# A second stage rewritten: tokens scattered into expert slots, one 4096-column tanh a step, sums shared by GpSimd and VectorE

## The chip, the core and the metric

One core of one Trainium2 chip. The metric is the device time of one execution in microseconds (us), median of several runs; lower is better. The engines are TensorE (PE in the profile; PEld is its weight load), VectorE (DVE), ScalarE (ACT), GpSimd (POOL) and the SyncE queue that issues transfers (SP).

## What is computed

Two layers over 2048 tokens (2 images of 32 x 32 positions) of 128 channels. The first is a 7 x 7 neighbourhood attention with a gate and a layer norm; the change does not touch how it is computed. The second, in two parts:

```
# additive attention, per image (L = 1024 keys, U = 32 units)
q = t @ Wt ; k = t @ Wx
h = tanh(q[:, :, None, :] + k[:, None, :, :] + bh)
e = h @ Wa + ba ;  a = softmax(e)
t = t + a @ layernorm(t)
# experts: E = 8, F = 512, capacity C = ceil(1.25 * 2048 / 8) = 320
x = layernorm(t) ; logits = x @ gate_w + gate_b
idx, prb = top-1 expert and its softmax probability
pos = rank of the token among those of its expert ; kept = pos < C
y = (relu(x @ w1[idx] + b1[idx]) @ w2[idx] + b2[idx]) * prb * kept
out = t + nan_to_num(y)
```

## The kernel before

The first layer runs in 32 half-block turns (`for rho in range(NR)`) and ends near 177 us. Then come 16 query blocks of 128 tokens, 8 for each image. The tanh of a block has 128 queries x 1024 keys x 32 units; four queries' units lie side by side in the 128 partitions, so that a block is 8 steps (`CH = 8`) of 4 x 1024 columns.

In a step, ScalarE's `hidden_units` does two tanh of 1024 columns straight from the keys, with the query as bias (L734), and one of 2048 columns (L736) whose sums GpSimd has prepared with two instructions of 1024 (L350, `key_query_sums`). TensorE's `energies` (L538) turns the step into energies: 8 f32 matmuls of 512 columns, each recorded as two. The keys of a block are staged by SP as copies in SBUF (`kcur`, `qcur`, `xcur`).

Blocks are pipelined. While block i makes its energies, block i-1 goes through softmax, transposes (L550), the product with the tokens (L561), the residual and the norm, and block i-2 through its experts: for each of the 8 steps one expert, with all 128 tokens of the block, four matmuls in (L575), a relu on VectorE (`hidden`, L1013), four matmuls out (L589) and a masked sum (`combine`, L1030). Every expert therefore sees every token, and a mask keeps one. The engines' programs are written out in order and meet by semaphores. Most blocks run in a hardware loop. The layer norm of the second image (`norm_part(1, ...)`, L851 to L871) runs on VectorE alongside the first block's tanh. `Chain` makes VectorE wait for its own last result. After the last energies the experts of the last three blocks run alone (`ahead`), with `finish` (L1037 to L1042) cleaning infinities and adding the residual.

## Time and profile before

| what | us |
|---|---|
| median of 3 runs | 794.61 (793.82 to 796.89) |
| the profiled execution | 795.25 |
| its span, first to last instruction | 793.0 |
| busy in the span: PE, DVE, ACT, POOL | 729.0, 530.6, 628.7, 292.0 |

The busy share is an average over three stages: the first layer, the 16 blocks, and a tail. In the rows below the number behind "x" is a count; a time in square brackets is idle time of the engine before the row and what ended it. [...]

### The profile page before, as it was taken

The numbers are of one execution on the slowest core, as the hardware profiler recorded it, in microseconds if no ns is written. First come the engines' busy times: TensorE is split into PE (matmuls) and PEld (weight loads), VectorE is DVE, ScalarE is ACT, GpSimd is POOL, SyncE is SP. The second block draws the span as 40 slices with busy tenths as digits, with TensorE's granted clock in tenths as the row PEclk, the third lists the DMA queues.
The fourth block names the chain that finished last, engine by engine and source line by source line (L and its number), as shares of the span: only waits on it lengthen the run. The fifth ranks groups of instructions, "written<-read, shape, count | busy, mean of one in ns | idle before, by whom it ended". The sixth has DMA issues, their size and how long they took to land.

```text
span 793.0 us, 16921 instructions
## 1 busy us (share of the span) xinstructions
PE 729.0 (92%) x6288; PEld 462.4 (58%) x6288; DVE 530.6 (67%) x1464; ACT 628.7 (79%) x661; POOL 292.0 (37%) x264
## 2 busy tenths in 40 slices
PE   6899998875698999999999999999999999999987
PEld 3666666651144666656665656656565656656686
DVE  2566798859725376675858576675858576675776
ACT  2367676659799998989999898989989898989500
POOL 1000000008545454545454454545454454545100
PEclk9799999999699999999999999999999999999999
DMA  9000000007001001010101001010101001010000
GB/s 323 12 2 2 1 2 2 1 11 310 1 1 55 30 26 58 0 57 0 57 0 57 29 28 57 0 57 0 57 0 57 19 38 57 0 57 0 3 5 7
DMA packets 11364, 29.38 MB, mean 37 GB/s; under 512 B 3264, under 2 KB 5312, under 8 KB 10688
## 3 DMA queue, kind: packets, MB, share of 16 engines
q1 hardware_dynamic: 11328, 28.91, 9.7%
q8 instruction: 22, 0.36, 0.2%
q14 instruction: 14, 0.11, 0.0%
HBM read 10.81 MB, written 1.05 MB: 15 GB/s over the span
## 4 chain that ended last, share of the span: by engine, by line
PE 61%; DVE 26%; issue 4%; ACT 3%; DVEq 0%; DMA 0%; SPq 0%; ACTq 0%
PE ps L538 19%; PE ps L589 14%; PE ps L575 10%; PE ps L561 4%; PE ps L413 3%; DVE hids L1013 3%; PE ps L426 2%; DVE sw L113 2%; PE ps L395 2%; DVE sw L114 2%; DVE nmin L954 2%; PE ps L550 2%; DVE arena L804 2%; DVE oha L992 2%; DVE sy L116 2%
## 5 line engine op out<-in xcount | busy, mean ns | idle before, releaser
L734 ACT ACTIVATE arena<-kcur,qcur 128x1024 f32<-128x1024 f32 x240 | 261.9, 1138 | 42.7 <-PE ps L538 42.6
L538 PE MATMUL ps<-arena,nwa 128*32 128x512 f32 x2048 | 252.2, 611 | 16.7 <-ACT arena L736 16.1
L350 POOL TENSOR_SCALAR early<-kcur,qcur 128x1024 f32<-128x1024 f32 x120 | 132.7, 1118 | 167.2 <-ACT arena L736 104.2
L589 PEld LDWEIGHTS ps<-arena,hids 128*128 128x128 f32 x1024 | 124.1, 191 | 93.6 <-issue 71.4
L350 POOL TENSOR_SCALAR tokens<-kcur,qcur 128x1024 f32<-128x1024 f32 x120 | 133.1, 1122 | 101.1 <-ACT arena L736 100.9
L589 PE MATMUL ps<-arena,hids 128*128 128x128 f32 x1024 | 146.4, 286 | 8.4 <-DVE hids L1013 7.0
L575 PE MATMUL ps<-xnT,arena 128*128 128x128 f32 x1024 | 136.5, 277 | 0.0
L1013 DVE TENSOR_TENSOR hids<-ps,nb 128x512 f32<-128x512 f32 x128 | 88.2, 689 | 67.6 <-PE ps L575 62.9
L575 PEld LDWEIGHTS ps<-xnT,arena 128*128 128x128 f32 x1024 | 124.4, 192 | 0.1
L538 PEld LDWEIGHTS ps<-arena,nwa 128*32 128x32 f32 x2048 | 54.5, 110 | 117.0 <-issue 82.1
L736 ACT ACTIVATE arena<-early 128x2048 f32<-128x2048 f32 x64 | 121.3, 1896 | 0.3 <-POOL early L350 0.3
L736 ACT ACTIVATE arena<-tokens 128x2048 f32<-128x2048 f32 x64 | 121.3, 1895 | 0.0
L1030 DVE SCALAR_TENSOR_TENSOR acc<-ps,msk,acc 128x128 f32<-128x128 f32 x112 | 39.1, 349 | 81.6 <-PE ps L589 78.3
L678 ACT ACTIVATE arena<-arena,mn 128x320 f32<-128x320 f32 (+1 forms) x128 | 62.7, 540 | 34.0 <-DVE mn L804 32.8
L350 POOL TENSOR_SCALAR early<-kT,tokens 128x1024 f32<-128x1024 f32 x8 | 11.4, 1438 | 174.7 <-DVE tokens L935 173.0
L804 DVE CUSTOM_DVE_ANT_0 arena<-ps,arena 128x320 f32<-128x320 f32 (+1 forms) x128 | 53.0, 470 | 16.1 <-PE ps L395 11.6
L413 PE MATMUL ps<-cst,arena 128*128 128x128 f32 x352 | 56.1, 292 | 3.5 <-ACT arena L685 3.5
L413 PEld LDWEIGHTS ps<-cst,arena 128*128 128x128 f32 x352 | 41.5, 150 | 13.5 <-ACT arena L685 6.3
L685 ACT ACTIVATE arena<-ps 128x512 f32<-128x512 f32 x56 | 33.0, 588 | 10.3 <-PE ps L413 10.3
L1041 DVE COPY_PREDICATED acc<-bad,fill 128x128 f32<-128x128 uint32 x48 | 36.1, 751 | 1.7
L561 PE MATMUL ps<-xcur,ptm 128*128 128x128 f32 x256 | 34.0, 276 | 0.0
L561 PEld LDWEIGHTS ps<-xcur,ptm 128*128 128x128 f32 x256 | 31.1, 192 | 0.4 <-issue 0.4
(133 smaller groups left out, 704.9 us busy)
## 6 DMA issues: line engine op xcount, KB each, us to landing
kcur<-kT SPq DMA_DIRECT2D x16, 512.0 KB, 2.9
xcur<-x_all SPq DMA_DIRECT2D x16, 512.0 KB, 3.2
arena<-in_w SPq DMA_DIRECT2D x2, 2048.0 KB, 11.1
arena<-in_inner SPq DMA_DIRECT2D x1, 1280.0 KB, 11.5
tokens<-in_xT SPq DMA_DIRECT2D x4, 256.0 KB, 6.4
arena<-in_top SPq DMA_DIRECT2D x1, 1024.0 KB, 7.4
arena<-in_bottom SPq DMA_DIRECT2D x1, 1024.0 KB, 15.7
out<-outs SPq DMA_DIRECT2D x16, 64.0 KB, 1.6
```

Source lines behind the costliest of these rows:

```text
L350: last = nc.gpsimd.tensor_scalar(kq_sum[s % 2][:, c, :], keys[:, :], queries[:, m:m + 1], 1.0, ALU.add, ALU.mult)
L413: last = nc.tensor.transpose(bank(to, g * P, (g + 1) * P), prob[r][:, g, c * P:(c + 1) * P], c_("ident"))
L538: last = nc.tensor.matmul(bank(2 * par + half)[c * U:(c + 1) * U, :], nwa[:, U - QPG - QPG * s:2 * U - QPG - QPG * s], hid_ring[s % 2][:, ...
L561: last = nc.tensor.matmul(bank(5, 0, C), ptm[:, k, :], xcur[par][:, k * C:(k + 1) * C], start=(k == 0), stop=(k == BPI - 1))
L575: last = nc.tensor.matmul(bank(0 if ahead and e % 2 else 6, c * P, (c + 1) * P), w1[:, e, c * P:(c + 1) * P], xnT[par][:, :], start=True, ...
L589: last = nc.tensor.matmul(bank(1 if ahead and e % 2 else 7, 0, C), hids[e % 2][:, c, :], w2[:, e, c, :], start=(c == 0), stop=(c == FC - 1))
L678: nc.scalar.activation(prob[r][:, g, 0:n], nlog[r][:, g, 0:n], ACT.Exp, bias=mn[r][:, g:g + 1], scale=-1.0).then_inc(p_ready, 1)
L734: nc.scalar.activation(hid_ring[s % 2][:, c, :], keys[:, :], ACT.Tanh, bias=queries[:, m:m + 1])
L736: nc.scalar.activation(hid_ring[s % 2][:, 2:4, :], kq_sum[s % 2][:, :, :], ACT.Tanh).then_inc(h_ready, 1)
L804: nc.vector.tensor_tensor_reduce(out=nlog[r][:, g, 0:n], in0=bank(g, 0, n), in1=btab[kind][:, 2 * g + r, :], scale=-1.0, scalar=3e38, op0= ...
L1013: nc.vector.tensor_tensor(hids[e % 2][:, :, :], bank(0 if ahead and e % 2 else 6).rearrange("p (c t) -> p c t", c=FC), nb1[:, e * FC:(e + ...
L1030: nc.vector.scalar_tensor_tensor(acc[:, :], out, w, acc[:, :], ALU.mult, ALU.add).then_inc(out_used, 1)
```

## The change

- Experts leave the block loop. Each block ends in a record of 272 columns a token (normed token, residual, 8 logits less their maximum, token number) and in a slot number (expert x 320 + rank). GpSimd scatters the record to its slot in a DRAM buffer of 2560 rows with one indirect transfer (`scatter`). SP has filled this buffer with blank records before.
- After the last block SP loads all slots back (4 transfers of 5 tiles of 128 slots), and the experts run once, each on its own 320 slots. GpSimd scatters the 20 tiles of results to the output rows; a blank slot's token number is out of bounds and writes nothing. SP has stored the residual rows to the output before.
- A step has one tanh of 4096 columns, in place in a ring of three buffers. All sums are made ahead: GpSimd the first 2.5 of the four 1024-column pieces, VectorE the last 1.5. Both read `k4`, both may start filling step t+3 when the energies of step t are done.
- The softmax sum comes from a column of ones beside the tokens; least and copy of the energies are one VectorE instruction; both blocks' energies use the same two PSUM banks, so the next block waits for `least_ready`. The logits and counts are f32.
- The loops over blocks are written out in full.

```diff
+T = NB * CH
 # gpsimd
-                for c in range(2):
-                    m = (2 + c) * CH + s
-                    last = nc.gpsimd.tensor_scalar(kq_sum[s % 2][:, c, :], keys[:, :], queries[:, m:m + 1], 1.0,
-                                                   ALU.add, ALU.mult)
+                else:
+                    pool.wait_ge(h_used, t - 2)
...
+                for c in range(3):
+                    n = L if c < 2 else L // 2
+                    m = i * U + c * CH + s
+                    last = nc.gpsimd.tensor_scalar(ring[t % 3][:, c, 0:n], k4[:, img * L:img * L + n], q4[:, m:m + 1],
+                                                   1.0, ALU.add, ALU.mult)
+                last.then_inc(pool_sums, 1)
...
+            for t in range(T):
+                i, s = divmod(t, CH)
+                if s == 6 and i >= 2:
+                    scatter(i - 2)
+                if t + 2 < T:
+                    key_query_sums(t + 2)
 # tensor
+                if s == 0 and i:
+                    pe.wait_ge(least_ready, i)
...
+            def first_product(e):
+                pe.wait_ge(xeT_ready, 2 * (e // 2) + 2)
                 for c in range(FC):
...
+                    nc.tensor.matmul(bank(c, 0, CAP), w1[:, e, c * P:(c + 1) * P], xeT[:, e * CAP:(e + 1) * CAP],
+                                     start=True, stop=True).then_inc(w1_done, 1)
...
+                for k, row, at, n in parts_of(e):
+                    to = slot_bank(k)
...
+                    for c in range(FC):
+                        last = nc.tensor.matmul(to[row:row + n, :], h[e % 2][:, c, at:at + n], w2[:, e, c, :],
+                                                start=(c == 0), stop=(c == FC - 1))
 # scalar
-                for c in range(2):
-                    m = c * CH + s
-                    nc.scalar.activation(hid_ring[s % 2][:, c, :], keys[:, :], ACT.Tanh, bias=queries[:, m:m + 1])
-                act.wait_ge(sum_ready, CH * i + s + 1)
-                nc.scalar.activation(hid_ring[s % 2][:, 2:4, :], kq_sum[s % 2][:, :, :], ACT.Tanh).then_inc(h_ready, 1)
+            def hidden_units(t):
+                act.wait_ge(pool_sums, t + 1)
+                act.wait_ge(dve_sums, t + 1)
+                nc.scalar.activation(ring[t % 3], ring[t % 3], ACT.Tanh).then_inc(h_ready, 1)
 # vector
+                for c in range(2, QPG):
+                    lo = L // 2 if c == 2 else 0
+                    m = i * U + c * CH + s
+                    last = nc.vector.tensor_scalar(ring[t % 3][:, c, lo:L], keys[:, lo:L], q4[:, m:m + 1], None, ALU.add)
+                last.then_inc(dve_sums, 1)
...
+            key_query_sums(0)
+            key_query_sums(1)
+            dve.wait_ge(y_ready, NB)
+            for t in range(T):
...
+                if t < 4:
+                    for part in range(4 * t, 4 * t + 4):
+                        norm_part(1, part)
...
+                if p >= 1 and s == 1:
+                    turned_normed(p - 1)
+                if p >= 1 and s == 3:
+                    route(p - 1)
+                if p >= 0 and s == 3:
+                    turned_main(p)
+                if p >= 1 and s == 5:
+                    slotted(p - 1)
+                if p >= 0 and s == 6:
+                    attended(p)
+                if p >= 0 and s == 7:
+                    normed(p)
+                if p >= 0 and s == 0:
+                    least(p)
+                if t + 2 < T:
+                    key_query_sums(t + 2)
 # sync
+            sp.wait_ge(h_used, T)
+            for i in range(2):
+                sp.wait_ge(scattered[i], 16 * NB // 2)
+            for q in range(NE // 2):
...
+                sp.dma_start(xe[:, q * n:(q + 1) * n, :], src).then_inc(ld_xe[q], 16)
```

After the experts' products, VectorE's `rectified` (L1153) does half of the relu, ScalarE the other half, and `slots_out` (L1164 to L1172) weighs, cleans and adds the residual for 2 or 3 tiles of slots at once.

How the order changes, first on GpSimd in the loop over blocks. Before, two steps of it (`early` and `tokens` are the two buffers of sums):

```order
L350 TENSOR_SCALAR early<-kcur,qcur 128x1024 x2
L346 REGISTER_ALU
L350 TENSOR_SCALAR tokens<-kcur,qcur 128x1024 x2
L346 REGISTER_ALU
L350 TENSOR_SCALAR early<-kcur,qcur 128x1024 x2
```

Now, the steps around a scatter (`arena` holds the ring, `xbuf` is the buffer in DRAM):

```order
L369 TENSOR_SCALAR arena<-k,q 128x1024 x2
L369 TENSOR_SCALAR arena<-k,q 128x512
L377 DMA xbuf<-rec,slots 2560x272
L369 TENSOR_SCALAR arena<-k,q 128x1024 x2
L369 TENSOR_SCALAR arena<-k,q 128x512
```

Each step has gained an instruction of 512 columns, and once in 8 steps the scatter's issue stands between two steps.

On VectorE, the part of a block at its steps 0 and 1. Before:

```order
L954 TENSOR_REDUCE nmin<-ps 128x1
L956 TENSOR_SCALAR nmin<-nmin,cst 128x1
L101 ISA
L1009 ISA
L1011 REGISTER_ALU
L1013 TENSOR_TENSOR hids<-ps,nb 128x512
L988 TENSOR_TENSOR lg<-ps,cst 128x8
```

Now, from step 0 to the routing of step 3 (the ISA row at L1019 is the combined copy and least of 1024 energies):

```order
L1019 ISA pm,nmin<-ps,cst 128x1024
L1019 ISA nmin 128x1
L1012 TENSOR_SCALAR arena<-k,q 128x512
L1012 TENSOR_SCALAR arena<-k,q 128x1024
L1059 COPY xnT<-ps 128x128
L1012 TENSOR_SCALAR arena<-k,q 128x512
L1012 TENSOR_SCALAR arena<-k,q 128x1024
L1012 TENSOR_SCALAR arena<-k,q 128x512
L1012 TENSOR_SCALAR arena<-k,q 128x1024
L1065 ISA lg,mx<-ps,cst 128x8
```

The relu and the masked sums of the experts have left; the two sums of every step have come, and they stand behind whatever the step's block work waits for.

## Rows read from the trace of the kernel before

**Rows 1.** Busy time by stage: stretch, PE, PEld, DVE, ACT, POOL busy (count), PEclk, DMA
```profile
0.00:177.00 177.00, 154.95 (x1592) 104.91 (x1592) 121.05 (x421) 102.64 (x214) 3.53 (x8) 0.94 0.11 39
177.00:251.28 74.28, 52.91 (x372) 19.73 (x372) 43.80 (x76) 66.84 (x53) 44.83 (x36) 0.89 0.26 100
251.28:749.32 498.04, 485.69 (x4027) 303.97 (x4027) 332.86 (x861) 457.26 (x390) 243.62 (x220) 1.00 0.08 30
749.32:793.00 43.68, 35.45 (x301) 33.74 (x300) 32.87 (x108) 1.99 (x6) 0.00 (x0) 0.99 0.02 6
```
**Rows 2.** Timeline of ScalarE: start, duration, line, what
```profile
190.93 1.89 ACT L736 ACTIVATE arena<-tokens 128x2048 f32<-128x2048 f32 x1
192.73 2.17 ACT L734 ACTIVATE arena<-kT,tokens 128x1024 f32<-128x1024 f32 x2
194.81 1.89 ACT L736 ACTIVATE arena<-early 128x2048 f32<-128x2048 f32 x1
...
255.49 1.09 ACT L742 ACTIVATE pm<-ps,nmin 128x1024 f32<-128x1024 f32 x1
```
**Rows 3.** GpSimd's sums in the loop over blocks, ns min/median/max
```profile
L350 POOL TENSOR_SCALAR tokens<-kcur,qcur x120: 1115/1118/1152, 208.5 to 737.0; 128x1024 f32<-128x1024 f32 x120
```
**Rows 4.** Timeline of VectorE, a norm part alone, then two beside GpSimd's sums
```profile
152.38 1.22 DVE L856 TENSOR_TENSOR tokens<-x_all 128x1024 f32<-128x1024 f32 x1
...
180.50 2.00 DVE L854 TENSOR_TENSOR y_all<-y_all,mean 128x1024 f32<-128x1024 f32 x1
...
181.40 4.14 POOL L350 TENSOR_SCALAR early<-kT,tokens 128x1024 f32<-128x1024 f32 x2
...
182.64 1.92 DVE L856 TENSOR_TENSOR tokens<-y_all 128x1024 f32<-128x1024 f32 x1
```
**Rows 5.** Groups of VectorE in the whole span: widths of short instructions
```profile
L1037 DVE TENSOR_TENSOR bad<-acc 128x128 uint32<-128x128 f32 x16 | 4.5, 281 | 0.0
...
L1038 DVE TENSOR_SCALAR bad<-acc 128x128 uint32<-128x128 f32 x16 | 3.6, 226 | 0.6
```
**Rows 6.** Timeline of VectorE: instructions of 8 columns, the second beside GpSimd's
```profile
207.32 0.17 DVE L115 TENSOR_SCALAR sw<-sw 128x8 f32<-128x8 f32 x1
...
431.54 0.94 DVE L991 TENSOR_SCALAR oha<-lg,mx 128x8 f32<-128x8 f32 x1
...
752.19 0.22 DVE L991 TENSOR_SCALAR oha<-lg,mx 128x8 f32<-128x8 f32 x1
```
**Rows 7.** Timeline of TensorE: energies of a step at either clock
```profile
189.00 1.93 PE L538 MATMUL ps<-arena,nwa 128*32 128x512 f32 x16 [1.96 <-ACT arena L736]
...
204.51 3.64 PE L538 MATMUL ps<-arena,nwa 128*32 128x512 f32 x16 [1.08 <-ACT arena L736]
```
**Rows 8.** Stretches inside the first blocks, columns as in rows 1
```profile
200.00:212.00 12.00, 6.44 (x32) 1.06 (x32) 10.87 (x19) 12.00 (x10) 7.81 (x6) 0.71 0.00 1
223.00:251.00 28.00, 24.68 (x214) 11.84 (x202) 7.49 (x25) 27.64 (x23) 15.02 (x14) 1.00 0.10 39
```
**Rows 9.** Timeline of VectorE: the norm of image two, first and last part
```profile
178.19 1.22 DVE L851 TENSOR_REDUCE mean<-y_all 128x8 f32<-128x1024 f32 x1
...
211.30 1.23 DVE L867 TENSOR_TENSOR x_all<-x_all,sy 128x1024 f32<-128x1024 f32 x1
```
**Rows 10.** The chain that ended last, in the tail: a piece of TensorE
```profile
776.00 0.89 PE ps L589 x8
```
**Rows 11.** Groups of VectorE used for the tail and the block work
```profile
L1041 DVE COPY_PREDICATED acc<-bad,fill 128x128 f32<-128x128 uint32 x48 | 36.1, 751 | 1.7
L963 DVE COPY ptm<-ps 128x512 f32<-128x512 f32 x32 | 21.7, 677 | 8.1 <-PE ps L550 8.1
L954 DVE TENSOR_REDUCE nmin<-ps 128x1 f32<-128x1024 f32 x16 | 19.4, 1214 | 0.0
```
**Rows 12.** Transfers of the page: KB each, us from issue to landing
```profile
arena<-in_w SPq DMA_DIRECT2D x2, 2048.0 KB, 11.1
...
out<-outs SPq DMA_DIRECT2D x16, 64.0 KB, 1.6
```

More of the change, by code:

```diff
@@ new lines, in counts @@
+            def counts(p):
+                pe.wait_ge(oh_ready, p + 1)
+                if p:
+                    pe.wait_ge(slot_ready, p)
+                at = bank(7, P + NE, P + 2 * NE)
+                nc.tensor.matmul(at, c_("tri"), oh[:, :], start=True, stop=False)
+                nc.tensor.matmul(at, ones[:, :], osum[:, :], start=False, stop=True).then_inc(cum_done, 1)
+            pe.wait_ge(ptd_ready, NR)
+            pe.wait_ge(pta_ready, chunks_before(NR) - NR)
+            pe.wait_ge(ots_ready, NB)
@@ new lines, in _, with turn_slots @@
+            p = NB - 1
+            turn_normed(p - 1)
+            logits(p - 1)
+            turn_main(p)
+            counts(p - 1)
+            attend(p, 0)
+            attend(p, 1)
+            turn_normed(p)
+            logits(p)
+            counts(p)
+            def turn_slots(q):
+                pe.wait_ge(ld_xe[q], 16)
+                if q:
+                    pe.wait_ge(xeT_ready, 2 * q)
+                for k in range(5):
+                    last = nc.tensor.transpose(bank(4 + k // 4, k % 4 * P, (k % 4 + 1) * P), xe[:, 5 * q + k, 0:C],
+                                               c_("ident"))
+                    if k >= 3:
+                        last.then_inc(xeT_done, 1)
@@ L661, in _ @@
+            pe.wait_ge(ld_w, 32)
+            pe.wait_ge(oh_ready, NB)
+            pe.wait_ge(slot_ready, NB)
+            pe.wait_ge(mt_ready, 2 * NB)
+            turn_slots(0)
+            first_product(0)
+            for e in range(NE):
+                if e % 2 == 0 and e + 2 < NE:
+                    turn_slots(e // 2 + 1)
+                if e + 1 < NE:
+                    first_product(e + 1)
+                second_product(e)
         @block.scalar
@@ L765, in _ @@
+            turned_slots(0)
+            weights(0)
+            rectified(0)
+            for e in range(NE):
+                if e % 2 == 0 and e + 2 < NE:
+                    turned_slots(e // 2 + 1)
+                    weights(e // 2 + 1)
+                if e + 1 < NE:
+                    rectified(e + 1)
         @block.vector
@@ new lines, in least, with turned_main @@
+            def least(p):
+                dve.wait_ge(h_used, CH * (p + 1))
+                if p:
+                    dve.wait_ge(mt_done, 2 * p)
+                nc.vector.tensor_tensor_reduce(out=pm[:, :], in0=ps[:, 0:L], in1=c_("ba").broadcast_to([P, L]),
+                                               scale=-1.0, scalar=3e38, op0=ALU.add, op1=ALU.min,
+                                               accum_out=nmin[:, :]).then_inc(least_ready, 1)
+            def turned_main(p):
+                for half in range(2):
+                    dve.wait_ge(mt_done, 2 * p + half + 1)
+                    if p and half == 0:
+                        dve.wait_ge(pvm_done, p)
+                    nc.vector.tensor_copy(ptm[:, 4 * half:4 * half + 4, :].rearrange("p k q -> p (k q)"),
+                                          bank(4 + half)).then_inc(mt_ready, 1)
@@ L1087, in _ @@
-            step_main(1, 1, moe=False, last=False)
-            dve.wait_ge(cx_done, NE)
-            nc.vector.tensor_tensor(cexp[:, :], bank(7, 0, C)[0:NE, :], c_("b2")[0:NE, :], ALU.add).then_inc(cx_ready, 1)
-            step_main(2, 0, last=False)
-            step_main(3, 1)
-            with dve.Fori(2, NB // 2) as n:
-                for par in range(2):
-                    step_main(2 * n + par, par)
-            step_main(NB, 0, ahead=True)
-            step_main(NB + 1, 1, attn=False, ahead=True, after=True)
@@ L1101, in _layouts @@
+            weights(0)
+            rectified(0)
+            for e in range(NE):
+                if e % 2 == 0 and e + 2 < NE:
+                    weights(e // 2 + 1)
+                if e + 1 < NE:
+                    rectified(e + 1)
+                slots_out(e)
 def _layouts(i):
```

740 lines of the change are left out of this document (353 added, 387 removed).

## The prediction

> **What bounds the kernel now.** I read the busy time by stage first [rows 1]. In the 14 blocks from 251.28 to 749.32 TensorE is busy 485.7 of 498.0 us, ScalarE 457.3, VectorE 332.9, GpSimd 243.6. A block takes 498.04 / 14 = 35.57 us, 4.45 a step: TensorE paces it. ScalarE is the next: two tanh of 1024 columns advance it by 194.81 - 192.73 = 2.08 us, one of 2048 by 192.73 - 190.93 = 1.80 [rows 2], so that a block of its work is 8 x 3.88 + 1.1 (the softmax's exp) = 32.1. Taking the experts out of the loop helps by no more than 3.4 us a block unless ScalarE's work falls too. So the sum is made over three parts: the blocks at their new pace, the start, and a tail that now holds all experts.
>
> **The change, part by part.**
>
> ScalarE: one tanh of 4096 columns. The slope of the two sizes is (1.80 - 1.04) / 1024 = 0.74 ns a column, so 1.80 + 2048 x 0.74 = 3.32 us a step, 3.4 to its end. With an exp of 1.0 a block is 8 x 3.32 + 1.0 = 27.6.
>
> TensorE: the expert matmuls leave. What stays is 1.93 us of energies a step [rows 7] and some 25 matmuls of 128 columns a block at 0.22 (see the tail), 5.5: 21 us of a block of 29 to 30, a load of 0.7. [...]
>
> GpSimd: 2.5 pieces a step instead of 2. By 1.12 us for 1024 columns [rows 3] that is 1.12 + 1.12 + 0.56 = 2.80 (the 512 taken as half).
>
> VectorE: sums of 512 and 1024 columns from SBUF to SBUF. No such instruction is in the trace. Bounds: a TENSOR_TENSOR of 1024 from SBUF takes 1.22 [rows 4]; but at 128 columns the TENSOR_SCALAR takes 226 ns where the TENSOR_TENSOR takes 281 [rows 5], and at 8 columns 170 [rows 6], a slope of 0.47 ns a column against 0.92. I take the lower slope, as it is the same kind of instruction: 0.17 + 0.05 for the pointer operand (0.22 against 0.17) gives 0.46 and 0.72 us.
>
> Both engines read SBUF, and the trace shows what that costs. The norm's TENSOR_TENSOR takes 1.22 alone and 2.00 and 1.92 beside GpSimd's sums, and GpSimd's two take 4.14 instead of 2.24 [rows 4]. They take turns: from the end of one norm part (182.50) to the next (184.56) lie 2.06 us, one instruction of each, while 1.22 + 1.12 = 2.34. So an exchange costs the sum less 0.28. The short TENSOR_SCALAR of 8 columns waits too, 0.94 where it takes 0.22 alone [rows 6], so a single input does not spare it. Then VectorE's sums add 0.46 - 0.28 + 0.72 - 0.28 = 0.62 to GpSimd's 2.80: **3.42 us a step** for the pair, against ScalarE's 27.6 / 8 = 3.45 with its exp. A block: 8 x 3.42 = 27.4, the scatter's issue, and six short VectorE instructions that also take a turn, 0.1 each, 0.6.
>
> [...]
>
> The scatter's issue on GpSimd is not in the trace. Nearest rows: a GpSimd instruction of 1.1 [rows 3], and a whole 64 KB transfer by SP in 1.6 from issue to landing [rows 12]. I take 1.2, with 0.5 and 3.3 (three instructions) as ends. [...]
>
> VectorE's own list in a block: 8 x 1.18 of sums, least and copy 1.3 (a reduce of 1024 takes 1.21), two copies at 0.68 [rows 11], and some 28 short instructions at about 0.2, 5.8: 17.9 us. Its waits for GpSimd, two a step and six more, at 0.5 to 1.0 each, add 11 to 20: 29 to 38 if GpSimd never paused. It does pause when VectorE is late, since its next fill waits for energies (`h_used`), and then VectorE's sums find the port free. I went through a block in turns: VectorE is late twice, at the least of step 0, which waits for the last energies of the block before and holds the next ones, and at the norm of step 7. Together some 0.4 a block. **29.6 us a block** (27.4 + 1.2 + 0.6 + 0.4), 3.70 a step, against 35.57. What was under cover and is no longer: the 6 short instructions and the scatter cost only because the pair paces.
>
> Start. The first layer to 177 is untouched; the blank records' store (2.8 MB) lies beside it. VectorE then does fills 0 and 1, each behind GpSimd's instructions, to about 183.8. The norm of image two took it from 178.19 to 212.53 [rows 9], 34.3, with GpSimd beside it, and now four fills of 2 us stand within: the fill of step 5 ends near 184 + 34 + 8 = 226. ScalarE has been starved until then. From 226 it does step 5 in 3.4 and 122 more steps, 15.25 blocks x 29.6 = 451.4: the last tanh ends at 681.
>
> Tail, from there. (a) The last two blocks to their slots, one chain: energies 1.9, least 1.3, routing of block 14 in VectorE's order before the copies, 3.5, copies and product 3, residual and norm 4, transpose, logits, routing, counts and slot 4.3: 18. (b) Last scatter 1.2 and landing 2.5: 3.7. (c) Reading 2.79 MB back: two loads of 2048 KB took 11.1 us [rows 12]; rows of 1088 bytes are shorter, the four queue behind each other: 9 to 18, I take 12. (d) Experts. Eight records of TensorE, which are four f32 matmuls of 128 columns, take 0.89 [rows 10], 0.22 each. An expert is 4 x 320 columns, 2.2, 12 matmuls of 128, 2.7, and 0.4 of transposes: 5.3. VectorE's share is two relus of 0.5, 2.5 products 1.0, three passes at 0.35, two sums 1.0, a COPY_PREDICATED 0.6 (0.33 at 128 alone, 0.75 on the mean [rows 11]), 0.2 of weights: 4.9. [...] (e) VectorE's last output 4.1, three scatters 3.6, landing 1.6: 9.3. Together 88. Before, the tail from 749.32 was 43.7, so it grows by 44 [rows 1].
>
> Sum: 226 + 3.4 + 451.4 + 88 = 768.8 of span. The profiled execution takes 2.25 more than its span, the median 0.64 less than that one, so 1.6 in all: **770 us**, 3.1% below 794.6.
>
> **The rivals.**
>
> *ScalarE paces* (the port costs little, 27.6 a block). For: 3.42 and 3.45 are a hair apart, and the ring of three lets the pair work ahead. Against: scatter and short instructions have no cover on GpSimd. 226 + 3.4 + 15.25 x 27.6 + 88 + 1.6 = 740.
>
> *The turns overlap in nothing; the pair costs 2.80 + 0.46 + 0.72 = 3.98 a step.* Slower than before. A block is 31.8 + 2.2 = 34.0, in all 226 + 3.4 + 518.5 + 88 + 1.6 = 837. For: half the exchanges here are of short instructions, of which no row shows the overlap. Against: the 2.06 of rows 4. It breaks even with 794.6 at 31.2 a block, 3.62 for the pair. With VectorE's sums at the TENSOR_TENSOR's 1.22 and 0.69, exchanges still overlapping, 2.80 + 1.22 + 0.69 - 0.56 = 4.15 a step give 859; the slope of rows 5 speaks against it. [...]
>
> *Indirect transfers are dear*, 3.3 us each on GpSimd. Loop: 2.1 x 15.25 = 32. Tail: the last slot 2, and 20 x 3.3 = 66 for the results instead of 45 beside the experts, 21. 770 + 55 = 825; at 2.2 each the tail is still covered and it is 770 + 15 + 4 = 789.
>
> *TensorE's clock falls* in steps without other work, as at 200 to 212, where 6.4 us were busy of 12 and the clock was 0.71 [rows 8]: then a step's energies take 3.64 [rows 7]. [...] A fall now and then costs 1.7, mostly within the ring's slack.
>
> **How the numbers follow.** Forecast as worked out, with the starting, loading and expert terms off by some us each way: 0.50, 750 to 790. ScalarE paces: 0.12, 740. No overlap, or slow VectorE sums: 0.13, 837 and up. Dear transfers: 0.17, of which half reaches past 799. Clock: 0.03, half of it past 799. The rest, 0.05, is several small terms adding up near 795. A measurement of this kernel can tell 0.5% (4 us) from no change. Faster: 0.50 + 0.12 + 0.06 + 0.02 = 0.70; within 0.5%: 0.07; slower: 0.23. The range 740 to 818 leaves out most of the no-overlap case, half of the dear transfers' and a bit below; the likeliest case's own is 750 to 790.
>
> **What would show it.** In the profile after: ScalarE's tanh at 3.4 us each; GpSimd's pairs of 1024 columns lengthened to about 1.6 by VectorE, three of them filling some 3.4 us; VectorE's L1012 at 0.46 and 0.72 alone and up to 1.1 more beside GpSimd; the least (L1019) every 29.6 us; ScalarE's idle time released by GpSimd's or VectorE's sums; step 5 starting near 226; the last tanh ending near 681; 88 us after it. Wrong would be: ScalarE without gaps (740), L1012 at 1.2 without GpSimd, gaps of GpSimd of 3 us around L377, PEclk of 0.5 in the loop, or a tail over 100.

## The result

The changed kernel takes 820.9 us at the median of 4 runs (818.98 to 822.94), the kernel before 794.2 beside it (793.52 to 796.89). The ratio is 1.033, 95% interval 1.029 to 1.037: 3.3% slower, where 3.1% faster was forecast. The time also lies above the upper end of the range, 818.

The page of the kernel after, by engine, with the groups that matter (line, engine, operation, count, busy us, mean ns, idle us before it and what ended it):

```profile
span 821.1 us, 11919 instructions
...
PE 562.9 (69%) x4436; PEld 268.8 (33%) x4436; DVE 646.8 (79%) x1326; ACT 584.9 (71%) x385; POOL 472.7 (58%) x453
...
L369 POOL TENSOR_SCALAR arena<-k,q 128x1024 f32<-128x1024 f32 (+1 forms) x384 | 423.3, 1119 | 279.9 <-DVE q L991 169.9
L781 ACT ACTIVATE arena<-arena 128x4096 f32<-128x4096 f32 x128 | 456.1, 3610 | 85.4 <-DVE arena L1012 72.9
...
L1012 DVE TENSOR_SCALAR arena<-k,q 128x512 f32<-128x512 f32 (+1 forms) x256 | 298.3, 1211 | 53.5 <-PE ps L586 45.6
...
L377 POOL DMA_INDIRECT xbuf<-rec,slots x16 | 17.8, 1115 | 25.7 <-DVEq L119 23.4
```

TensorE no longer paces: it was busy 485.7 of 498 us in [rows 1]. No engine does for long. ScalarE's tanh waits 72.9 us for VectorE's sums. The busy time by stage (columns as in rows 1), the first block after the start and the blocks behind it:

```profile
229.00:258.00 29.00, 19.45 (x161) 6.42 (x161) 22.21 (x37) 29.00 (x10) 27.99 (x26) 1.00 0.01 3
261.00:731.00 470.00, 307.81 (x2218) 107.40 (x2210) 407.48 (x665) 407.51 (x125) 374.11 (x342) 0.88 0.02 7
```

In the first, ScalarE is busy all of 29.0 us and TensorE's granted clock (PEclk, 1.00 being full speed) is 1.00. It is the only one of the blocks between two leasts that has neither a scatter nor a routing. Behind it ScalarE is busy 407.5 of 470 us, and the granted clock is 0.88 on the mean; a step's energies take 1.92 us in some steps and 3.62 in others, as the rows below show. VectorE's least marks the blocks, here by its least, median and highest duration in ns, its first and its last start:

```profile
L1019 DVE CUSTOM_DVE_ANT_0 pm<-ps,cst x16: 1205/1210/1225, 228.7 to 731.1; 128x1024 f32<-128x1024 f32 x16
```

That is (731.1 - 228.7) / 15 = 33.5 us a block, where 29.6 was forecast. Singly the starts lie 29.6 us apart for the first block and 33.4 to 36.0 for those from the second to the last but one. So the first block came out as forecast, and something in the next ones costs 4 us more. The timeline of one block's border, of GpSimd, then VectorE, then TensorE (start, duration, idle time before it; the last row shows the first 8 of its 16 matmuls):

```profile
411.13 7.06 POOL L369 TENSOR_SCALAR arena<-k,q 128x1024 f32<-128x1024 f32 x6 [1.15 <-PE ps L586]
418.35 1.00 POOL L377 DMA_INDIRECT xbuf<-rec,slots  x1 [0.16 <-issue]
419.40 9.17 POOL L369 TENSOR_SCALAR arena<-k,q 128x1024 f32<-128x1024 f32 x9
```
```profile
419.08 6.09 DVE L1012 TENSOR_SCALAR arena<-k,q 128x512 f32<-128x512 f32 x2
...
428.18 1.33 DVE L1012 TENSOR_SCALAR arena<-k,q 128x512 f32<-128x512 f32 x2 [0.18 <-DVE rec L1051]
429.43 1.21 DVE L1019 CUSTOM_DVE_ANT_0 pm<-ps,cst 128x1024 f32<-128x1024 f32 x1
...
430.57 1.14 DVE L1012 TENSOR_SCALAR arena<-k,q 128x512 f32<-128x512 f32 x2
```
```profile
407.39 3.62 PE L586 MATMUL ps<-arena,cst 128*32 128x512 f32 x16 [2.28 <-ACT arena L781]
...
421.95 1.92 PE L586 MATMUL ps<-arena,cst 128*32 128x512 f32 x16 [1.58 <-ACT arena L781]
428.14 0.47 PE L618 MATMUL ps<-cst,rec 128*128 128x128 f32 x1 [4.27 <-DVEq L119]
430.80 1.93 PE L586 MATMUL ps<-arena,cst 128*32 128x512 f32 x8 [2.19 <-DVE nmin L1019]
```

A row x2 of L1012 holds both of VectorE's sums of a step, one over 512 and one over 1024 keys. This pair takes 1.14 us alone (430.57) and 6.09 beside the nine sums that GpSimd runs in a row behind its scatter. VectorE's norm and its least stand behind that pair, TensorE waits 4.27 and 2.19 us for them, and then the ring of three is full: GpSimd and VectorE both stop for TensorE. The waits of the loop from 261 to 700 us (who, for whom, us, times, longest):

```profile
POOL arena L369 <- PE ps L586: 82.0, 21, 6.4
PE ps L586 <- ACT arena L781: 75.0, 53, 2.8
...
ACT arena L781 <- DVE arena L1012: 47.9, 24, 3.6
PE ps L618 <- DVEq L119: 47.1, 12, 4.4
DVE arena L1012 <- PE ps L586: 37.7, 25, 2.6
PE ps L586 <- DVE nmin L1019: 27.1, 12, 2.3
```

### The profile page after: what moved, and what is told of

Its sections match the earlier page's. It is cut to its first block, busy times and chain, and to the rows that moved or that the text cites. A ratio compares the mean times of both kernels' runs of the same rounds, so it can differ in the third digit from the quotient of the medians.

```text
span 821.1 us, 11919 instructions
## 1 busy us (share of the span) xinstructions
PE 562.9 (69%) x4436; PEld 268.8 (33%) x4436; DVE 646.8 (79%) x1326; ACT 584.9 (71%) x385; POOL 472.7 (58%) x453
## 4 chain that ended last, share of the span: by engine, by line
DVE 45%; PE 23%; issue 12%; ACT 8%; POOL 6%; DMA 1%; DVEq 0%; POOLq 0%; ACTq 0%; SPq 0%
DVE arena L1012 21%; PE ps L586 10%; ACT arena L781 8%; POOL arena L369 4%; PE ps L460 3%; PE ps L473 2%; DVE rec L1051 2%; PE ps L442 2%; POOL out L405 2%; DVE pm L1019 2%; DVE arena L864 2%; DVE sw L142 1%; DVE osum L1083 1%; DVE sy L143 1%; PE ps L499 1%
## 5 line engine op out<-in xcount | busy, mean ns | idle before, releaser
L369 POOL TENSOR_SCALAR arena<-k,q 128x1024 f32<-128x1024 f32 (+1 forms) x384 | 423.3, 1119 | 279.9 <-DVE q L991 169.9
L781 ACT ACTIVATE arena<-arena 128x4096 f32<-128x4096 f32 x128 | 456.1, 3610 | 85.4 <-DVE arena L1012 72.9
L586 PE MATMUL ps<-arena,cst 128*32 128x512 f32 x2048 | 288.1, 694 | 148.9 <-ACT arena L781 119.2
L1012 DVE TENSOR_SCALAR arena<-k,q 128x512 f32<-128x512 f32 (+1 forms) x256 | 298.3, 1211 | 53.5 <-PE ps L586 45.6
L586 PEld LDWEIGHTS ps<-arena,cst 128*32 128x32 f32 x2048 | 63.7, 122 | 324.6 <-ACT arena L781 178.9
L736 ACT ACTIVATE arena<-arena,mn 128x320 f32<-128x320 f32 (+1 forms) x128 | 62.7, 539 | 34.1 <-DVE mn L864 32.9
L609 PE MATMUL ps<-x_one,ptm 128*128 128x129 f32 x256 | 39.2, 300 | 2.0 <-DVE ptm L1028 2.0
L609 PEld LDWEIGHTS ps<-x_one,ptm 128*128 128x128 f32 x256 | 33.5, 204 | 15.5 <-issue 12.6
L873 DVE COPY arena<-ps 128x512 f32<-128x512 f32 x32 | 22.0, 688 | 8.0 <-PE ps L460 8.0
L473 PE MATMUL ps<-arena 128*32 128x128 f32 x704 | 27.3, 287 | 1.1
L701 PE MATMUL ps<-arena 128*128 128x128 f32 (+1 forms) x192 | 24.1, 278 | 0.7 <-issue 0.7
```

Of the source, the lines that this page charges most:

```text
L369: last = nc.gpsimd.tensor_scalar(ring[t % 3][:, c, 0:n], k4[:, img * L:img * L + n], q4[:, m:m + 1], 1.0, ALU.add, ALU.mult)
L473: last = nc.tensor.matmul(bank(6, r * P, (r + 1) * P)[g * HP:(g + 1) * HP, :], vals[:, value_block(j, c), 2 * g + r, :], pts[r][:, c, g * ...
L586: last = nc.tensor.matmul(bank(half)[c * U:(c + 1) * U, :], c_("wa", U - QPG - QPG * s, 2 * U - QPG - QPG * s), ring[t % 3][:, c, half * 5 ...
L609: last = nc.tensor.matmul(bank(6, 0, C + 1), ptm[:, k, :], x_one[:, p // BPI * BPI + k, :], start=(k == 0), stop=(k == BPI - 1))
L701: last = nc.tensor.matmul(to[row:row + n, :], h[e % 2][:, c, at:at + n], w2[:, e, c, :], start=(c == 0), stop=(c == FC - 1))
L736: nc.scalar.activation(prob[r][:, g, 0:n], nlog[r][:, g, 0:n], ACT.Exp, bias=mn[r][:, g:g + 1], scale=-1.0).then_inc(p_ready, 1)
```

## The experiments

All are edits of the changed kernel; times are medians of four runs (but for `no_dve_sums`, one run), ratios are to the kernel before run beside them on the same chip. "Block" is the mean distance of VectorE's 16 leasts.

**First, is it the turns of GpSimd and VectorE at SBUF, or the order of work at the border?** The prediction and the expectations call what the two take turns at the port. The traces show the turns (an instruction of 1.22 us took 2.00 and 1.92 beside GpSimd's sums in rows 4), not what makes them. `psum_keys` takes VectorE's keys from PSUM, with the keys of image two multiplied once more into banks 2 and 3:

```
-                keys = k4[:, i // BPI * L:(i // BPI + 1) * L]
+                keys = ps[:, 2 * 512:4 * 512]
...
+                if t == BPI * CH - 2:
+                    pe.wait_ge(dve_sums, BPI * CH)
+                    key_rows(1, (2, 3))
```

> VectorE's sums read the keys from PSUM banks 2 and 3 (the product stays there for image one, and is made a second time for image two); GpSimd still reads them from SBUF. Theory P (the SBUF port pair, which the two engines take in turns, sets the block): no instruction of the sums waits for the other engine. L1012 would be constant near 0.75 and 1.28 us, longer than alone from SBUF but without waits; VectorE's block list is then 25 us, GpSimd's 24, and ScalarE's 8 x 3.51 + 1.0 = 29.1 paces: 30 us a block instead of 33.5, kernel 765 to 772 us. Theory O (the order of the work at a block's border holds TensorE: it waits for the norm of step 7 and the least of step 0, whatever the port does): VectorE does the same list in the same order and takes longer a sum, so TensorE's waits of 4.0 and 2.3 us a block stay: 32 us or more a block, kernel 800 us or more.

761.1 us, ratio 0.959 (0.956 to 0.961): faster than both kernels, and a little below what theory P gave. `no_dve_sums` leaves VectorE's sums out from step 3 on:

```
+                if t >= 3:
+                    dve.sem_inc(dve_sums, 1)
+                    return
```

> Leaves out VectorE's sums from step 3 on (their 1.5 pieces keep what the last tanh left there, so the output is not the reference's); everything else runs. Upper bound of what the sums on VectorE cost, port and list together. Both P and O: 29.1 to 29.6 us a block, ScalarE without gaps, kernel 757 to 765 us. If a block stays over 32, neither holds, and TensorE's clock or the scatters set the pace.

754.9 us, just under its range. `late_two` keeps the sums at SBUF and eases the order instead: transposes of the normed tokens, logits, counts, slots and scatter each one step later, and the energies of odd blocks in banks 2 and 3, so that they needn't wait for the least:

```
-                if s == 6 and i >= 2:
+                if s == 7 and i >= 2:
                     scatter(i - 2)
...
-                    nc.tensor.matmul(bank(half)[c * U:(c + 1) * U, :],
+                    nc.tensor.matmul(bank(i % 2 * 2 + half)[c * U:(c + 1) * U, :],
```

> The border of a block loosened, the port left as it is: TensorE transposes the normed tokens one step later (and logits, counts, routing, slots and scatter one step later each), and energies of odd blocks go to banks 2 and 3, so that they do not wait for the least of the block before. Theory O: TensorE's waits for the norm (51 us in all) and for the least (29 us) go, a block falls from 33.5 to near the 29.7 that exchange of the port and scatter add up to, kernel 765 to 775 us. Theory P: VectorE still waits for two or three of GpSimd's instructions at a time, only elsewhere; ScalarE goes on idling 4 us a block behind L1012; 32.5 us a block or more, kernel 805 us or more.

835.8 us, ratio 1.052 (1.050 to 1.055), slower still: the theory of the order falls. In the groups of `psum_keys` ScalarE paces, both sizes of VectorE's sums take one time each, and so do GpSimd's:

```profile
L784 ACT ACTIVATE arena<-arena 128x4096 f32<-128x4096 f32 x128 | 451.2, 3606 | 27.3 <-DVE arena L1017 27.3
L369 POOL TENSOR_SCALAR arena<-k,q 128x1024 f32<-128x1024 f32 x256 | 284.0, 1122 | 269.4 <-DVE q L994 168.9 <-PE ps L586 99.1
...
L1017 DVE TENSOR_SCALAR arena<-ps,q 128x1024 f32<-128x1024 f32 x128 | 163.2, 1275 | 0.0
L1017 DVE TENSOR_SCALAR arena<-ps,q 128x512 f32<-128x512 f32 x128 | 96.0, 750 | 67.5 <-PE ps L586 58.3 <-PE ps L557 5.8 <-DVE rec L1056 2.9
L369 POOL TENSOR_SCALAR arena<-k,q 128x512 f32<-128x512 f32 x128 | 89.5, 699 | 0.0
```

**Second, the scatter or the sharing as such?** The long waits stand beside the scatter in every block, and in `late_two` they moved a step with it. `no_scatter` leaves the 16 transfers out and keeps the wait for the slots; `plain_scatter` makes them ordinary ones, from the same place of GpSimd's queue. It tells whether the indirect form puts VectorE's two next sums back, or whether any transfer issued there does it:

```
-                nc.gpsimd.indirect_dma_start(xbuf_d, bass.IndirectOffsetOnAxis(ap=slots[i % 2][:, :], axis=0),
...
+                pool.sem_inc(scattered[i % 2], 16)
...
+                nc.gpsimd.dma_start(xbuf_d[i * P:(i + 1) * P, :], rec[i % 2][:, :]).then_inc(scattered[i % 2], 16)
```

> The changed kernel with its 16 scatters of tokens left out (GpSimd only signals that they are done), so the experts read empty slots and the output is not the reference's. In the changed kernel the two VectorE sums that stand next to GpSimd's scatter wait 1.6 and 2.3 us, through two and three GpSimd sums, in every block, and every other sum waits for one at most. Theory S (the issue of the indirect transfer on GpSimd sets this off, and without it the two engines take turns as forecast): both waits fall under 1 us, the first instruction of VectorE's least comes each 29.7 to 30.3 us where it came each 33.5, TensorE's mean clock goes to about 0.94, and the time falls by 14 x 3.5 and the two transfers of the tail, to 760 to 775 us. Theory R (the crowd at the block's border does it: VectorE's list is longest there, and the scatter only stands beside it): the waits stay at that step, the block loses the 1.1 us of the issue at most, 32.4 to 33, and the time is 800 to 812 us.

> The changed kernel with each of its 16 indirect transfers replaced by an ordinary transfer of the same record to rows in order, issued from GpSimd's queue at the same place; the slots are not used, so the output is not the reference's. [...] If any transfer issued from GpSimd does it, the two waits of 1.6 and 2.3 us stay, the block stays at 33 to 33.6 and the time at 812 to 822 us.

Without scatters 759.9 us, ratio 0.957 (0.955 to 0.959), and a block of 29.0, with VectorE's and GpSimd's sums at SBUF as before. Ordinary transfers: 827.4 us, above even the 812 to 822 that were expected if any transfer does it. So 16 instructions of 1.1 us cost 61 us, and their being indirect has no part in it. Up to the end of the last tanh it is 67 us (729.1 against 661.9); the tail of `no_scatter` takes 4 us longer than that of the kernel after, by a gap of another kind (see the tail below). In `no_scatter` ScalarE paces, without a gap (columns as in rows 1):

```profile
261.00:660.00 399.00, 268.89 (x2193) 97.26 (x2193) 366.55 (x662) 399.00 (x125) 369.67 (x327) 1.00 0.01 3
```

`sp_scatter` sends the same ordinary transfers from SyncE's queue, `extra_sum` puts a GpSimd sum of 1024 columns where the scatter stood:

> The changed kernel with the 16 records sent by ordinary transfers from SyncE's queue, to rows in order and not by slots, so the output is not the reference's; GpSimd issues none in the loop. An ordinary transfer issued from GpSimd at its old place gave 827 us, none at all 760. If it is the issue on GpSimd that puts VectorE back, this gives 760 to 764; if it is the reading of the record by the DMA engines beside the sums, it stays at 810 to 827.

> The changed kernel with each of its 16 scatters replaced by one more sum over 1024 keys on GpSimd (1.12 us, into a place that nothing reads), at the same place of GpSimd's queue and behind the same wait for the slots; the tokens are not scattered, so the output is not the reference's. Theory S (the transfer's issue on GpSimd puts VectorE back): as without the scatter, 760 us, plus at most what the extra sum costs VectorE's turn, 760 to 768. Theory D (GpSimd's second of delay and its wait for the slots bring its nine sums into one row behind it, and that row starves VectorE): the waits of 2 and 2.4 us stay and the time is 810 to 822.

756.3 us from SyncE, a little under its range: the traffic costs nothing here (759.9 without any), the issue on GpSimd does (827.4). With the extra sum 779.0, ratio 0.979 (0.976 to 0.982), more than theory S had put (760 to 768) and far from D: one more instruction of GpSimd costs 19 us in all, since the pair has next to no slack, and the remaining 42 belong to the issue. The durations of VectorE's sums tell the two apart (ns, least/median/highest), in `no_scatter`, in `plain_scatter` and in three kernels described below, `scatter_s3`, `scatter_moved` and `scatter_s5`:

```profile
L1010 DVE TENSOR_SCALAR arena<-k,q x256: 472/1176/1622, 175.1 to 654.9; 128x512 f32<-128x512 f32 x128
```
```profile
L1010 DVE TENSOR_SCALAR arena<-k,q x256: 471/1177/4746, 175.8 to 719.7; 128x512 f32<-128x512 f32 x128
```
```profile
L1013 DVE TENSOR_SCALAR arena<-k,q x256: 468/1175/3760, 177.2 to 714.6; 128x512 f32<-128x512 f32 x128
```
```profile
L1013 DVE TENSOR_SCALAR arena<-k,q x256: 471/1175/6682, 177.0 to 686.0; 128x512 f32<-128x512 f32 x128
```
```profile
L1013 DVE TENSOR_SCALAR arena<-k,q x256: 471/1178/9550, 175.8 to 718.9; 128x512 f32<-128x512 f32 x128
```

Without an issue no sum takes over 1.62 us, the 0.74 of its own and one wait of at most 0.88. With one it takes up to 3.4 (after), 3.8, 4.7, 6.7 or 9.6. The last is one sum that waited through all nine of GpSimd's. In the kernel after too the longest wait is of this kind; it strikes the last multiply of a norm, which takes 0.34 us alone (GpSimd's row behind the issue, then VectorE's):

```profile
317.80 8.57 POOL L369 TENSOR_SCALAR arena<-k,q 128x1024 f32<-128x1024 f32 x9
```
```profile
319.57 6.89 DVE L1051 TENSOR_SCALAR rec<-rec,mv,sy 128x128 f32<-128x128 f32 x1
```

That block is the longest of all, 36.0 us.

**Third, which of the sums, and where?** `psum_big` takes only the sums over 1024 keys from PSUM, `psum_once` both sums, but only in step 0 of blocks 2 to 15:

> Only VectorE's sum over 1024 keys reads PSUM (1.28 us); its sum over 512 keys still reads SBUF. If the port between the two engines costs by the number of instructions that want it, the one that is left still has to wait out one or two GpSimd sums beside the scatter, 1.1 to 2.3 us once a block, and less than ScalarE's slack hides the rest: block 29.1 to 30.5, time 761 to 780 us. If the size of VectorE's SBUF work counted, the saving of 0.74 of 1.22 us a step would leave a third of the loss: block 30.5 to 31, time 775 to 790.

> Nothing left out: VectorE reads the keys from PSUM only for the sums of step 0 of blocks 2 to 15 (14 of 128 steps: 2.0 us instead of 1.2 and the waits of 4.2), those that stand beside the scatter; the other 114 steps take turns at SBUF as in the changed kernel. Theory S: the loss sits in these two sums, so nearly all of it goes, 760 to 768 us. If the lost turns only wait for the next SBUF sum (step 1) and come back there, 785 to 815.

`psum_big` gives 777.2 us, inside both of its time ranges. Its block tells them apart: 29.8 us lies in the first (29.1 to 30.5) and not in the second (30.5 to 31), which speaks for a cost by the number of VectorE's instructions that have to take a turn. One starved sum a block is left instead of two, in 12 of 13 blocks, with 2.2 us of wait. `psum_once` gives 809.2, against theory S as it stood. The two sums beside the issue go through in 1.94 us, and in nine of 13 blocks the next pair that wants SBUF, 5 us after the issue, is starved in their place (in one more it is the norm's multiply; in the first three nothing is). VectorE's sums in its timeline:

```profile
406.01 1.94 DVE L1018 TENSOR_SCALAR arena<-ps,q 128x512 f32<-128x512 f32 x2
411.65 3.96 DVE L1018 TENSOR_SCALAR arena<-k,q 128x512 f32<-128x512 f32 x2 [0.19 <-DVE rec L1057]
```

GpSimd had issued at 405.27 and ran nine sums in a row to 415.1. So the state can outlast the issue. Three kernels move the scatter, each with the tokens of one block earlier so that the slots are long ready, to step 1 (`scatter_moved`, shown), 3 (`scatter_s3`) and 5 (`scatter_s5`):

```
-                if s == 6 and i >= 2:
-                    scatter(i - 2)
+                if s == 1 and i >= 3:
+                    scatter(i - 3)
```

> Nothing left out: each scatter stands three steps later in GpSimd's queue (step 1 of the next block instead of step 6), where its slots have long been ready. By theory S VectorE's two waits of 1.8 and 2.4 us go with it, from step 0 to step 3 of each block. Whether that helps hangs on what VectorE has beside them: its list is shortest at steps 1 and 2, where every one of its sums now goes through without a wait. If the slack there takes half of the 4.2 us, 785 to 805 us; if none, 812 to 822; if the loss was only at the full border, 762 to 775.

> Nothing left out: the scatter stands before GpSimd's sums for step 5 of the next block, where the pair takes turns one for one. If what a scatter costs is GpSimd's time at the port alone (1.0 to 1.3 us a block, since the pair paces), the time is 760 + 15 to 20 = 775 to 780 us wherever it stands off the border, and VectorE never waits for more than one sum. If every issue makes VectorE lose two to three turns where it wants SBUF, 785 to 800.

> Nothing left out: the scatter stands before GpSimd's sums for step 7, one step of its queue ahead of the old place but with slots that have long been ready. If the neighbourhood of the block's border (VectorE's copies, residual, norm and least between its sums) is what makes it dear, 800 to 820 us; if only the wait for fresh slots made it so, 775 to 785.

Step 1: 786.0 us, ratio 0.989 (0.987 to 0.992), inside its first range, but not by the slack that the range was put down to, as the rows show. Step 3: 824.4, outside both of its ranges. Step 5: 825.1, also above both; the wait for fresh slots is not it. Two rows of GpSimd and one of VectorE for each, `scatter_s3` and `scatter_moved`:

```profile
399.69 1.00 POOL L377 DMA_INDIRECT xbuf<-rec,slots  x1 [0.16 <-issue]
400.74 9.34 POOL L369 TENSOR_SCALAR arena<-k,q 128x1024 f32<-128x1024 f32 x9
```
```profile
400.67 9.96 DVE L1013 TENSOR_SCALAR arena<-k,q 128x512 f32<-128x512 f32 x4
```
```profile
416.75 1.00 POOL L377 DMA_INDIRECT xbuf<-rec,slots  x1 [0.16 <-issue]
420.23 6.38 POOL L369 TENSOR_SCALAR arena<-k,q 128x1024 f32<-128x1024 f32 x5 [2.48 <-PE ps L587]
```
```profile
420.15 2.02 DVE L1013 TENSOR_SCALAR arena<-k,q 128x512 f32<-128x512 f32 x2 [1.71 <-PE ps L587]
```

In the first, GpSimd goes on at once and without a pause: VectorE gets three sums done in 9 us, one for each three of GpSimd's. In the second, GpSimd pauses 2.5 us behind the issue for TensorE, and the pair takes turns one for one afterwards (2.02 us for two sums). In `scatter_moved` 10 of the 13 scatters with sums behind them have such a pause, and no sum is starved there. The other three have none, and two of them bring the sums of up to 6.7 us. That makes a theory that can be tested alone: break the row. `scatter_pause` adds one wait behind the scatter:

```
                     scatter(i - 2)
+                    pool.wait_ge(dve_sums, min(t + 3, T))
```

> Nothing left out and nothing moved: behind each scatter of the loop GpSimd now waits for VectorE's two sums of the step that it would fill next, so that it pauses once instead of running nine sums in a row. Theory S2 (from a transfer's issue until GpSimd's next pause VectorE gets the port once in three of GpSimd's sums, and a pause ends that): no sum of VectorE waits for more than one of GpSimd's in the rest of the block, the two next to the scatter not at all; what is left is GpSimd's own delay, the issue and a pause of 1 to 2 us a block, partly made good by its idle 6 us: 775 to 795 us, though GpSimd works later. If the state were tied to time after the issue or to the work at the border and not to the unbroken row, VectorE's sums behind the pause would wait 1.8 to 3 us again and the time would be 815 to 840.

770.2 us (767.02 to 776.88), ratio 0.968 (0.965 to 0.971), 51 us faster than the changed kernel by one added wait, and below even what was expected. The profiled execution is the slowest of the four. GpSimd's row and VectorE's sums around it:

```profile
399.17 1.00 POOL L377 DMA_INDIRECT xbuf<-rec,slots  x1 [0.16 <-issue]
401.17 19.73 POOL L369 TENSOR_SCALAR arena<-k,q 128x1024 f32<-128x1024 f32 x18 [1.00 <-DVE arena L1013]
```
```profile
399.90 1.17 DVE L1013 TENSOR_SCALAR arena<-k,q 128x512 f32<-128x512 f32 x2
403.64 2.21 DVE L1013 TENSOR_SCALAR arena<-k,q 128x512 f32<-128x512 f32 x2 [0.18 <-DVE rec L1052]
```

After a pause of 1.0 us the row is 18 sums long, twice as long as in the kernel after, and starves nobody: the highest duration of a VectorE sum is 1.62 us again. So a long row alone does no harm, an issue with a pause behind it does none, and the two together do.

The timelines of all kernels can be counted through. Each has 13 scatters in the loop with sums of GpSimd behind them. "Starved" is an instruction of VectorE that takes over 1.62 us, which none does in the loop without an issue.

| VectorE's sums | GpSimd behind the issue | starved |
|---|---|---|
| both at SBUF (after, tail_pool, late_two, plain_scatter, scatter_s3, scatter_s5) | goes on at once | 78 of 78 |
| both at SBUF, scatter_moved | goes on at once | 2 of 3 |
| in part at PSUM (psum_big, psum_once) | goes on at once | 22 of 26 |
| both at SBUF (scatter_moved, scatter_pause) | pauses 1.0 us or more | 0 of 23 |
| both at SBUF (no_scatter, extra_sum, sp_scatter) | no issue | none |

The exceptions are few, but they show that an issue with an unbroken row is not always enough; what decides there is open. A shorter pause later in the row ends the state as well: in `plain_scatter` GpSimd stops for 0.12 us behind its sixth sum in 11 of the 13 blocks, and the starved sum (4.7 us) gets its turn there.

**Last, the tail, and the two gains together.** `tail_pool` lets GpSimd's third and fourth group of bias products stand behind the output scatters of experts 1 and 3, no longer ahead of all of them:

```
             for e in range(NE):
                 pool.wait_ge(y_out, e + 1)
+                if e in (1, 3):
+                    biases((e + 3) // 2)
```

> Only GpSimd's order behind the last block changes: the last two groups of bias products (L397) stand between the output scatters of experts 1 and 3 instead of ahead of all of them. In the changed kernel the 20 output scatters begin at 791.7, only when the last weights are ready, and run 1.28 us each to 817.9, while the results of the last expert are ready at 808.8. Expected: the last three scatters start at the last result, 808.8 + 3 x 1.28 + 2 = 814.6 instead of 821.1, kernel 6 to 7 us shorter, blocks unchanged at 33.5. If the transfers themselves or VectorE ended the kernel, no change.

> Two changes together: VectorE's sums read the keys from PSUM (alone 761.1 us), and GpSimd's last two groups of bias products stand between the output scatters (alone 3.5 us less than the changed kernel at the median, 4.9 in the span). The places do not meet, so the gains add: 755 to 758 us, 0.950 to 0.955 of before. If the tail's gain was only a different start of the tail, 760 to 762.

`tail_pool`: 817.4 us, 3.5 less than the changed kernel's median (4.9 in the span), a smaller gain than expected. The intervals of the two ratios all but touch (1.024 to 1.030 and 1.029 to 1.037); the tails behind the last tanh show the gain better, 87.6 us for 92.0, and 88.1 in `psum_tail` for 92.8 in `psum_keys`. `psum_tail`, with the keys from PSUM as well: 758.1 us, ratio 0.954 (0.951 to 0.957), the fastest kernel that leaves nothing out, 4.6% below the kernel before.

| kernel | median us | ratio to before | block us |
|---|---|---|---|
| after | 820.9 | 1.033 | 33.5 |
| late_two / tail_pool | 835.8 / 817.4 | 1.052 / 1.027 | 34.3 / 33.4 |
| no_dve_sums | 754.9 | 0.950 | 29.1 |
| plain_scatter / sp_scatter | 827.4 / 756.3 | 1.042 / 0.952 | 33.2 / 29.1 |
| no_scatter / extra_sum | 759.9 / 779.0 | 0.957 / 0.979 | 29.0 / 30.8 |
| scatter at step 1 / 3 / 5 | 786.0 / 824.4 / 825.1 | 0.989 / 1.039 / 1.036 | 30.9 / 32.9 / 33.2 |
| scatter_pause | 770.2 | 0.968 | 29.8 |
| psum_once / psum_big / psum_keys | 809.2 / 777.2 / 761.1 | 1.019 / 0.979 / 0.959 | 32.1 / 29.8 / 29.3 |
| psum_tail | 758.1 | 0.954 | 29.3 |

`no_dve_sums` leaves out VectorE's sums; `no_scatter`, `extra_sum`, `plain_scatter` and `sp_scatter` leave out the sorting of the tokens into slots.

## Why the prediction was wrong

The forecast's span was 768.8, the measured one 821.1, 52.3 more. Step 5's tanh starts at 215.6 instead of 226: -10.4. From there to the end of the last tanh at 729.1 it takes 513.5 instead of 454.8: +58.7. The tail takes 92.0 instead of 88: +4.

**The block, 29.6 forecast, 33.5 measured.** Its terms one by one:

- *The pair's turns, 3.42 a step.* Right in kind, though in `no_scatter` it is ScalarE that paces (399.0 us busy of 399.0), with the pair close behind it. A VectorE sum takes 0.48 and 0.74 us alone, as taken (0.46, 0.72), and waits for one GpSimd sum at most (0.88) in the whole of `no_scatter`. GpSimd's sum over 512 takes 0.70 alone and not the 0.56 of "half"; 8 times that is 1.1 us a block too little.
- *ScalarE, 27.6.* The slope of 0.74 ns a column was too low. The tanh takes 3.61 us, and six in a row, here in `psum_keys`, advance ScalarE by (21.14 - 3.61) / 5 = 3.51 each:

```profile
643.98 21.14 ACT L784 ACTIVATE arena<-arena 128x4096 f32<-128x4096 f32 x6
```

  So a block is 8 x 3.51 + 1.0 = 29.1. This is the pace of `no_scatter`, `sp_scatter` and `psum_keys` (29.0 to 29.3), and the first block's 29.0 without a gap. The rival at 740 was thereby out of reach. The forecast's 29.6 was nearly right for a block without the scatter's harm, and by luck: two of its terms were low, and it took the pair for the one that paces.
- *The scatter's issue, 1.2.* This is the step that failed. The issue itself lasts 1.0 to 1.1 us, but with it a block is 33.5 and without it 29.0: the term is 4.5 us, of which only some 1.8 is GpSimd's time (`extra_sum`, 30.8). The prediction counted what GpSimd spends on the issue and not what the issue does to the order of the turns.
- *"VectorE is late at the least and the norm, some 0.4 a block".* The place was right and the size was not. Here the 4 us come out: the pair of sums ahead of the norm takes 6.09 us, norm and least come late by that, and TensorE and then both engines at the ring wait for them. Going through a block by hand assumed that VectorE gets its turn at the end of each GpSimd sum. Behind an issue it got it once in three of them, or not until the row had ended.

**The rivals.** *No overlap of the turns* (34.0 a block, 837) came near the block's size by another mechanism: `no_scatter` has all the sharing and none of the loss. With turns that overlap in nothing, a step would cost the sum of its five instructions alone, 1.12 + 1.12 + 0.70 + 0.48 + 0.74 = 4.16 us, a block 33.3; `no_scatter` takes 29.0, so the runs speak against it, as rows 4 did. *Dear indirect transfers* named the right instruction but the wrong price: at 1.0 us busy and 1.28 apart in the output scatters they are cheap, and an ordinary transfer did as much harm. *The clock*: 0.88 in the loop and 1.00 in that of `no_scatter` (261 to 660 us), with the same matmuls. TensorE was busy 268.9 of 399.0 us there, and 19.45 of 29.00 at a clock of 1.00 in the first block of the kernel after. That its longer waits are why the clock fell is the author's estimate. In the rows above a step's energies take 3.62 us at 407.39, where the granted clock is 0.53, and 1.92 at 421.95, where it is 1.00. What share of the 4.5 us comes through that is open; no run held the clock up alone.

**Start.** Step 5 came 10.4 us earlier, and the timeline of the kernel after says where. Fills 0 and 1 ended at 180.9 instead of 183.8 (2.9). Eight us had been put down for the four fills of VectorE at the norm; they took 2.30, 1.15, 1.15 and, up to the tanh's start, 2.2, together 6.8 (1.2). The norm of image two itself took 27.9 for 34.3 (6.4): GpSimd stood idle for 5.9, 3.7 and 4.3 us beside it, waiting for TensorE, and most of the norm's instructions then ran at the 1.22 us that they take alone. That this idle time is the reason is argued, not tested.

**Tail.** (a) 21.3 for 18 to the last slots. (b) and (c) the scatter and the reading back 6.3 for 15.7: the last record lands 2.1 us after its issue, the four transfers of 680 KB are all in 9.8 us after the first was issued (for 12), but the experts start on the first of them, which lands after 4.1. (d) 2.1 to the first expert's product and 45.4 from there, for 45. The 45 were 42 for eight experts at 5.3, 1 for the weights and first relu, and 2 for a slow clock after the idle time; no run shows these 2 us as such, only a granted clock of 0.72 from 758 to 766 us and of 1.00 from 766 to 800. (e) 16.9 for 9.3, an order that the prediction had not followed out: every bias product stands ahead of the first output scatter in GpSimd's queue, as its timeline in the kernel after shows.

```profile
789.76 1.76 POOL L397 TENSOR_SCALAR arena<-arena,prb 128x128 f32<-128x128 f32 x5 [9.10 <-DVEq L119]
791.68 1.17 POOL L405 DMA_INDIRECT out<-ye,dest  x1 [0.16 <-issue]
...
816.90 0.97 POOL L405 DMA_INDIRECT out<-ye,dest  x1 [0.30 <-issue]
```

Twenty issues at 1.28 us then run on past the last expert. The error is in what is moved past which queue, and it is worth 7.6 us by the terms, of which `tail_pool` got back some 4.5.

In six of the kernels (`no_scatter`, `plain_scatter`, `psum_big`, `scatter_s3`, `scatter_s5`, `scatter_pause`) GpSimd stands idle for 6.0 to 7.7 us once among its last output scatters, which it does not in the kernel after. Their tails take 96.3 to 101.0 us, those of the others 87.6 to 93.5. The cause is open, and a difference of a few us between two of these kernels can come from it alone.

## What to carry to other kernels

Where GpSimd and VectorE both read SBUF without slack, look at what else GpSimd issues. Here a transfer of 1.1 us a block made a block 4.5 us longer (33.5 for 29.0): it cost what VectorE lost until GpSimd next paused, and what stood behind VectorE's next sums. Four ways out were measured, against 820.9 us: to issue it just ahead of a place where GpSimd waits anyway (`scatter_moved`, 786.0), to make such a place with a short wait for VectorE's sums (`scatter_pause`, 770.2; 1.0 to 1.8 us of wait a block brought back 51 of 61 us), to send it from another engine if its addresses allow (`sp_scatter`, 756.3, with ordinary transfers), or to give one of the two its operand from PSUM (`psum_keys`, 761.1). When a pace is made of turns, work out who gets the next turn after each odd instruction, and not only the sum of the durations.

## What the runs showed of the hardware

- Taking turns one for one (`no_scatter`), a VectorE sum waits at most 0.88 us for GpSimd's, and GpSimd's 1.12 becomes up to 1.55. Behind the issue of a transfer on GpSimd, indirect or ordinary, if its sums follow without a pause, VectorE got its turn only once in three of them (single sums of 3.4 and 3.8 us), only behind the sixth (4.7 and 6.7) or not before the end of all nine (9.6). This lasted for as long as the row did, nine sums or some 9 us in most blocks, also where VectorE's two sums beside the issue read PSUM (`psum_once`). It happened behind 102 of 107 such issues, behind none of 23 with a pause of 1.0 us or more (`scatter_moved`, `scatter_pause`), and nowhere without an issue. Why the turns change is not shown; the runs show only when they do.
- The same 16 ordinary transfers give 756.3 us from SyncE's queue and 827.4 from GpSimd's; without any it is 759.9.
- VectorE's TENSOR_SCALAR over 1024 f32 takes 0.74 us from SBUF and 1.28 from PSUM, over 512 0.48 and 0.75. The dearer source was the faster kernel (761.1 us for 820.9).
- In the kernel after, an indirect transfer's issue on GpSimd takes 1.0 to 1.3 us, 1.28 from one to the next among the output scatters; ScalarE's tanh over 4096 columns in place 3.61 us, over 2048 before 1.89.
